# The first feed-forward of a two-layer kernel: another order of its turns and joins, one group of bias products per step, both norms on ScalarE

## The reference

```python
x = layernorm(x + attn0(x))              # 16 heads of 16, causal; ctx @ Wp.T + bp
# first feed-forward, 8 experts, top 2, all experts computed for all tokens:
probs = softmax(x @ router_w + router_b)
gates = top-2 of probs, divided by their sum, 0 elsewhere          # (tokens, 8)
expert_out = gelu(x @ expert_w[e] + expert_b[e])                   # tanh form
x = layernorm(x + (sum_e gates[:, e] * expert_out[e]) @ out_w + out_b)
x = layernorm(x + attn1(x));  x = layernorm(x + ffn1(x))
layernorm(x) = (x - mean) / sqrt(var + 1e-5)
```

## Time and profile before

| | |
|---|---|
| median of 3 runs | 1004.56 us (1003.43 to 1004.66) |
| the profiled execution's own time | 1002.59 us |
| its span, first to last instruction | 1000.7 us |
| mean granted TensorE clock | 0.969 of full speed |
| busy, share of the span | PE 89%, PEld 54%, DVE 72%, ACT 51%, POOL 38% |
| first expert product to last one before the second attention's scores | 280.9 to 454.0 us |

### The profile page before, as it was taken

How to read it: one execution, slowest core, us unless ns; L and a number is a source line. 1 busy time by engine, 2 the same in 40 slices (tenths; PEclk the granted TensorE clock), 3 DMA queues, 4 the chain that set the end, 5 groups by cost and what they waited for, 6 DMA issues and landing times.

```text
span 1000.7 us, 22546 instructions
## 1 busy us (share of the span) xinstructions
PE 889.1 (89%) x8457; PEld 540.2 (54%) x8457; DVE 717.9 (72%) x1955; ACT 515.4 (51%) x1201; POOL 381.5 (38%) x729
## 2 busy tenths in 40 slices
PE   5897989997488989988999999999999999898796
PEld 2444544553334444345565676676667666676464
DVE  4776777676467786758999888888888888422646
ACT  3566657765224343436666555555555655314342
POOL 3543444544335545442333332333233333100455
PEclk8899999999779999999999999999999999999999
DMA  7233222320000000003667565556565555300011
GB/s 268 83 81 85 66 54 65 87 29 7 1 1 1 1 1 1 1 1 68 118 124 122 98 103 97 105 99 102 92 107 98 101 99 99 67 1 1 1 43 43
DMA packets 210428, 65.64 MB, mean 66 GB/s; under 512 B 203008, under 2 KB 206608, under 8 KB 210192
## 3 DMA queue, kind: packets, MB, share of 16 engines
q1 hardware_dynamic: 210320, 64.19, 32.4%
HBM read 17.92 MB, written 4.19 MB: 22 GB/s over the span
## 4 chain that ended last, share of the span: by engine, by line
PE 58%; DVE 17%; ACT 7%; issue 6%; POOL 5%; DMA 5%; SPq 1%; POOLq 0%; DVEq 0%; ACTq 0%
PE bank L411 13%; PE bank L413 12%; PE bank L412 12%; DMA att<-w_lo 4%; PE bank L755 3%; ACT scr L890 3%; PE bank L538 3%; PE bank L757 3%; PE bank L756 3%; DVE scr L1167 2%; ACT att L936 2%; PE bank L459 2%; POOL scr L1706 2%; DVE w_lo L1249 2%; DVE stats L1295 1%
## 5 line engine op out<-in xcount | busy, mean ns | idle before, releaser
L980 ACT ACTIVATE att<-att,nm 128x512 f32<-128x512 f32 (+3 forms) x256 | 141.5, 553 | 103.8 <-DVE nm L1238 102.5
L411 PE MATMUL bank<-w_hi,scr 128*128 128x256 bf16 (+1 forms) x576 | 174.2, 302 | 17.0 <-DVE scr L1167 14.3
L413 PE MATMUL bank<-w_hi,scr 128*128 128x256 bf16 (+1 forms) x576 | 173.8, 302 | 0.0
L412 PE MATMUL bank<-w_lo,scr 128*128 128x256 bf16 (+1 forms) x576 | 173.6, 301 | 0.0
L890 ACT ACTIVATE scr<-bank 128x256 bf16<-128x256 f32 (+3 forms) x208 | 110.4, 550 | 113.4 <-PE bank L757 44.6
L1167 DVE TENSOR_TENSOR scr<-bank,scr 128x256 bf16<-128x256 f32 (+1 forms) x144 | 75.2, 536 | 73.3 <-ACT scr L890 73.1
L1238 DVE CUSTOM_DVE_ANT_0 att<-bank,consts 128x512 f32<-128x512 f32 (+3 forms) x256 | 113.3, 483 | 15.0 <-PE bank L413 15.0
L936 ACT ACTIVATE att<-bank 128x512 f32<-128x512 f32 (+1 forms) x192 | 90.6, 525 | 61.3 <-PE bank L522 60.7
L1225 DVE TENSOR_REDUCE nm<-bank 128x1 f32<-128x512 f32 (+3 forms) x256 | 110.4, 483 | 13.7 <-PE bank L483 13.2
L1741 POOL TENSOR_SCALAR wqkv_hi<-att,rr 128x512 bf16<-128x512 f32 (+3 forms) x128 | 65.6, 532 | 139.0 <-DVE rr L1255 139.0
L1741 POOL TENSOR_SCALAR w_hi<-att,rr 128x512 bf16<-128x512 f32 (+3 forms) x128 | 65.6, 532 | 105.1 <-DVE rr L1255 105.1
(11 more groups left out here) (177 smaller groups left out, 2129.4 us busy)
## 6 DMA issues: line engine op xcount, KB each, us to landing
scr<-wall_in SPq DMA_DIRECT2D x19, 512.0 KB, 4.9
x_tok<-x_tok_in SPq DMA_DIRECT2D x1, 2048.0 KB, 9.4
v_by_token<-scr SPq DMA_DIRECT2D x16, 128.0 KB, 1.8
scr<-v_by_token SPq DMA_DIRECT2D x16, 128.0 KB, 3.3
scr<-x_t_in SPq DMA_DIRECT2D x3, 512.0 KB, 5.9
out<-x_tok SPq DMA_DIRECT2D x3, 512.0 KB, 3.0
scr<-wqkv_in SPq DMA_DIRECT2D x2, 384.0 KB, 3.6
att<-w_hi SPq DMA_TRANSPOSE x32, 3.4
```

The lines of the kernel that those rows point to most:

```text
L411: pe.matmul(out, l_hi, r_hi, start=start, stop=False, skip_group_check=check)
L412: pe.matmul(out, l_hi, r_lo, start=False, stop=False, skip_group_check=check)
L413: return pe.matmul(out, l_lo, r_hi, start=False, stop=stop, skip_group_check=check)
L980: last = act.activation(at, at, ACT.Exp, bias=nm[:, j % 2, qt:qt + 1], scale=-1.0, accum_out=rs[:, j % 2, qt:qt + 1])
```

## The change

It does six things. (1) The four bias products of a step become one group, behind the six products of `experts(n, 0)`: each takes its own quarter of the array's rows (32 q to 32 q + 2), three of them open the banks of calls 1 to 3, the last closes bank 4. PE waits for all four gelus of the step before ahead of the group. (2) The bias rows therefore lie at four partition offsets, and SP moves them with 12 DMAs in place of 3. (3) The turns come in the order x1, cc, cm, x2. PE: x1, experts 0 with the group, first_project, experts 1, cc, experts 2, cm, experts 3, x2, second_project. (4) DVE's order is new: low x1, mix 0, joined 2 of tile n-2 (one step later than before), join_halves(n-1) (moved from the end of the step before), joined 1, low cc, mix 1, low cm, mix 2, context, low x2. (5) Both norms go from DVE (subtract, multiply) to ACT (one activation, scale 1/sqrt, bias -mean/sqrt), norm 1 before gelu 2 and norm 2 before gelu 3; POOL computes the bias with a third small instruction per norm, and does norm 2's numbers first in a step. (6) The router's exponential goes between gelu 0 and gelu 1.

```diff
-TURN_LEADS = (("x1", LEAD), ("x2", -2), ("cm", -1), ("cc", LEAD + 2))
+TURN_LEADS = (("x1", LEAD), ("cc", LEAD + 2), ("cm", -1), ("x2", -2))
...
-            for i in range(3):
-                sp.dma_start(eb3[i:i + 1, :], eb_p[:, i, :]).then_inc(eb_moved, 16)
+            for p in range(4):
+                for i in range(3):
+                    sp.dma_start(eb3[32 * p + i:32 * p + i + 1, :], eb_p[4 * p:4 * p + 4, i, :]).then_inc(eb_moved, 16)
...
             def experts(t, p):
-                hold(pe, m["ge"], 4 * (t - 1) + p + 1)
                 out = bank[4 + p][:, :]
-                pe.matmul(out, ones_b[0:3, :], eb3[:, p * 512:(p + 1) * 512], start=True, stop=False)
+                if p == 0:
+                    hold(pe, m["ge"], 4 * (t - 1) + 1)
                 for k in range(KE):
...
-                               w_hi[:, cs], w_lo[:, cs], False, k == KE - 1)
+                               w_hi[:, cs], w_lo[:, cs], p == 0 and k == 0, p > 0 and k == KE - 1)
+                if p == 0:
+                    hold(pe, m["ge"], 4 * t)
+                    for q in (1, 2, 3, 0):
+                        rows = slice(32 * q, 32 * q + 3)
+                        last = pe.matmul(bank[4 + q][:, :], ones_b[rows, :], eb3[rows, :], start=(q > 0), stop=(q == 0),
+                                         tile_position=(32 * q, 0))
                 last.then_inc(m["f"], 1)
...
# ACT, new; norm(t, which) is gone from DVE, where it was one tensor_scalar
+            def norm(t, which):
+                rows = x_tok[:, t * E:(t + 1) * E]
+                slot = 2 * (which - 1) + t % 2
+                act.wait_ge(m[f"rstd{which}"], t + 1)
+                act.activation(rows, rows, ACT.Identity, bias=shift[:, slot:slot + 1], scale=rstd[:, slot:slot + 1]
+                               ).then_inc(m[f"x{which}"], 1)
...
# ACT, a step after: x1 high, gelu 0, [router_exp], gelu 1, cc high, norm(n+6, 1), gelu 2,
#                    cm high, norm(n-2, 2), gelu 3, x2 high
+                if 0 <= n + LEAD + 1 < NT:
+                    norm(n + LEAD + 1, 1)
+                if here:
+                    gelu(n, 2)
+                if 0 <= n - 1 < NT:
+                    turned_high("cm", n - 1)
+                if 0 <= n - 2:
+                    norm(n - 2, 2)
...
# DVE, a step after
                 if here:
                     mix(n, 0)
+                if 0 <= n - 2:
+                    joined(n - 2, 2)
+                if 0 <= behind < NT:
+                    join_halves(behind)
                 if 0 <= ahead < NT:
                     joined(ahead, 1)
...
# POOL
+            def scale_and_shift(t, which):
+                pool.wait_ge(m[f"agg{which}"], t + 1)
+                mix_chain(pool.tensor_scalar(var_e[:, col], mv[:, slot, 1:2], EPS, 1.0, ALU.add, ALU.mult))
+                hold(pool, m[f"x{which}"], t - 1)
+                mix_chain(pool.tensor_tensor(rstd[:, col], var_e[:, col], neg_half[:, one], ALU.pow))
+                pool.tensor_scalar(shift[:, col], mv[:, slot, 0:1], rstd[:, col], -1.0, ALU.mult, ALU.mult
+                                   ).then_inc(m[f"rstd{which}"], 1)
             def mix_step(n):
+                if 0 <= n - 2:
+                    scale_and_shift(n - 2, 2)
                 if 0 <= n + LEAD + 1 < NT:
+                    scale_and_shift(n + LEAD + 1, 1)
                 if 0 <= n < NT:
                     mix(n, 2)
...
                     pool.tensor_tensor(rows, rows, outb_bc[:, :], ALU.add).then_inc(m["xb"], 1)
+                if 0 <= n < NT:
+                    mix(n, 3)
```

More of the change, by code:

```diff
@@ L689, in _ @@
                     experts(n, 0)
-                if 0 <= n + 4 < NT and (n + 4) % TT == TT - 1:
+                routed = 0 <= n + 4 < NT and (n + 4) % TT == TT - 1
+                if routed:
                     logits((n + 4) // TT)
-                if 0 <= n - 2:
-                    turn_mix("x2", n - 2)
-                routed = 0 <= n + 4 < NT and (n + 4) % TT == TT - 1
                 if 0 <= ahead < NT and not routed:
@@ L710, in _ @@
                 if 0 <= behind < NT:
-                    second_project(behind)
+                    turn_mix("cm", behind)
                 if n == NT:
@@ L715, in _ @@
                     experts(n, 3)
+                if 0 <= n - 2:
+                    turn_mix("x2", n - 2)
+                if 0 <= behind < NT:
+                    second_project(behind)
             l1_project("q", 0, 1)
@@ L964, in l0_slot @@
                         if 0 <= n + LEAD:
+                            norm(n + LEAD, 1)
                             turned_high("x1", n + LEAD)
@@ L1295, in joined @@
                 chain(dve.bn_stats(stats[:, slot, :], rows))
+                hold(dve, m[f"rstd{which}"], t - 1)
                 dve.bn_aggr(mv[:, slot, :], stats[:, slot, :]).then_inc(m[f"agg{which}"], 1)
-            def norm(t, which):
-                rows = x_tok[:, t * E:(t + 1) * E]
-                slot = 2 * (which - 1) + t % 2
-                dve.wait_ge(m[f"rstd{which}"], t + 1)
-                dve.tensor_scalar(rows, rows, mv[:, slot, 0:1], rstd[:, slot:slot + 1], ALU.subtract, ALU.mult
-                                  ).then_inc(m[f"x{which}"], 1)
             def sums_inverse(half):
@@ L1371, in join_halves @@
                 dve.wait_ge(m["psum"], (NX - DVE_X - 1) * (t + 1))
-                dve.wait_ge(m["mul"], MIX * t + DVE_X)
-                dve.tensor_tensor(comb[t % 2], comb[t % 2], pc[t % 2], ALU.add).then_inc(m["mul"], 1)
+                dve.wait_ge(m["mul"], DVE_X * (t + 1))
+                dve.tensor_tensor(comb[t % 2], comb[t % 2], pc[t % 2], ALU.add).then_inc(m["join"], 1)
             def route(b):
@@ L1440, in _ @@
                     mix(n, 1)
-                if 0 <= ahead < NT:
-                    norm(ahead, 1)
-                if 0 <= behind < NT:
-                    joined(behind, 2)
                 if routed:
                     choose_first((n + 4) // TT)
+                if 0 <= behind < NT:
+                    turned_low("cm", behind)
+                if n == NT:
+                    l1_low("v", 0)
                 if here:
                     mix(n, 2)
+                if routed:
+                    choose_second((n + 4) // TT)
+                    gate((n + 4) // TT)
                 if 0 <= n + LEAD + 3 < NT:
                     context(n + LEAD + 3)
-                if n == NT:
-                    l1_low("v", 0)
-                if 0 <= behind < NT:
-                    norm(behind, 2)
-                if routed:
-                    choose_second((n + 4) // TT)
-                if routed:
-                    gate((n + 4) // TT)
-                if here:
-                    join_halves(n)
+                if 0 <= n - 2:
+                    turned_low("x2", n - 2)
             l1_low("q", 0, 1)
@@ L1694, in mix @@
                 if p == 2:
-                    hold(pool, m["mul"], MIX * (t - 1))
+                    hold(pool, m["join"], t - 1)
                     if t % TT == 0:
```

63 lines of the change are left out of this document (25 added, 38 removed).

## The result

| | before | after |
|---|---|---|
| median (lowest to highest) | 1003.99 us of 6 runs (1002.44 to 1005.36) | 1008.35 us of 6 runs (1007.62 to 1010.28) |
| the profiled execution's own time, its span | 1002.59, 1000.7 | 1007.9, 1006.0 |
| mean granted TensorE clock | 0.969 | 0.955 |

A forecast was written before the change was run, and what follows sets the result against it. The prediction took a loop through PE, gelu 3, POOL and DVE's join as the bound, 10.4 us a full step. Feed-forward -9.1, issues +5.6 and first norm -1.6 gave -5.1, so 1004.56 became 999.5 us, range 990 to 1009.

The forecast's parts named there:

- The new loop: Full feed-forward steps: gelu 0, DVE's joins, POOL, norm 1, gelu 2, norm 2, x2 turn, experts 0; 10.4 us a step.
- the four bias products run side by side: PE's group in each step: 0.4 us in place of 1.64, a gain of 1.2 of PE's time a step.
- nine more issues: SP's bias-row DMAs at the start of the feed-forward: last landing 9 x 0.62 = 5.6 us later.
- rival 4: Start of the feed-forward: the additional DMA issues cost nothing, 994 us; chance 0.08.
- I keep one fall of the clock as before saw it, 1.3: Feed-forward steps: one clock fall of 1.3 us kept, turning 10.4 us less into 9.1 less.
- rival 1: PE's gaps before x2: clock falls in steps 2 to 9, 1.5 x 8 = 12 us, giving 1010; chance 0.18.
- the gain at the start: Early steps: first norm on ACT takes 0.5 plus 0.3 for POOL's third instruction, against 2.42 on DVE; 1.6 us less.
- the later early norms: Early steps, norms after the first: moving them to ACT comes out even.
- the last routed pair: Feed-forward steps 11 and 12, with routing: forecast at 17.5 us together.
- the old loop: Kernel before, join to join through PE, gelu 3, POOL and DVE: 10.38 us, with four bias products costing 1.64.
- The forecast's price for the new order: Feed-forward to the second attention: 162.7 against 173.1 us, 10.4 less; 9.1 less after one clock fall.
- the end: Steps 13 to 15 and the way to the second attention: 34.3 us against 36.2.

The follow-up runs named there:

- three_issues: The change with the bias rows moved by three strided DMAs in place of twelve; 1002.99 us, 0.9984 of the kernel before.
- fill_gap: The change with twelve idle 256-column products on PE ahead of the x2 turn in each step from n = 2; 1004.34 us, 0.9998 of the kernel before.
- group_only: The kernel before with only the bias products as a group of four and SP's twelve issues; 1007.46 us, 1.0027 of the kernel before, expected about 997.
- norm1_late_and_wait: The change with norm 1 behind norm 2 on ACT and PE's bias-row wait just ahead of the first group; 978.47 us, 0.9739 of the kernel before.
- best: The change with norm 1 behind norm 2, the bias-row wait ahead of the first group, and joined 1 ahead of joined 2 and the join; 987.26 us, 0.9825.
- join_moved_only: The kernel before with only the join of tile n-1 moved behind mix 0 of step n; 1008.16 us, 1.0038 of the kernel before.

## Why the prediction failed

The measured 1008.35 us lie just inside the range of 990 to 1009, which was to take in a clock that falls in most gaps. The direction was wrong: faster had a chance of 0.63, slower 0.26.

**Right.** The new loop, its links and its length (10.25, forecast 10.4) and that PE would stand still before x2 (2.1 to 2.6 us, forecast 2.6). That the four bias products run side by side (0.40). That nine more issues cost 5.6 (5.5 in the trace, 6.3 by three_issues), and rival 4, that they cost nothing, is refuted. Without clock falls the steps come out almost as summed: 0 to 9 were forecast at 103.5 us, and fill_gap takes 102.8.

**Wrong, the largest step:** "I keep one fall of the clock as before saw it, 1.3". In after the clock falls behind the gaps of steps 2, 4, 8 and 9 and behind one of 2.42 us in step 11, not behind those of steps 3, 5, 6 and 7, and the falls before step 10 alone took 5.9 us, by fill_gap. This is rival 1 at half its price: it put a fall into each of eight steps and 1.5 us on each. The rows had shown one fall in two such gaps; that rate times eight gaps of 1.5 us is 6, close to what came, though two gaps are too few to give a rate and the match is partly luck. The forecast took one fall for all eight gaps. (By its own numbers the sign turns at the fifth such fall, not at the fourth: 4 x 1.5 - 1.3 is 4.7, less than 5.1.)

**Right in mechanism, halved by the clock: the gain at the start.** Forecast 1.6 less; it was 0.85 less in the change's profile and 1.65 in that of three_issues, whose clock fell there as in before. Another 0.5 was lost again by step 0: the norm on ACT took 0.60, not 0.5, and the shift (0.27) stands ahead of it. The forecast had the later early norms come out even.

**Wrong: the last routed pair.** Steps 11 and 12 were forecast at 17.5 and took 19.9. PE waits 2.42 us there, ahead of 416.11, for the low part of cm behind DVE's router pieces, a wait that the sum had left out for this step, and the fall of the clock follows it. With the clock full and the gap filled in part, fill_gap ran step 11 1.7 us faster, so most of the 2.4 is the fall.

**Wrong, without effect on the sum: the old loop.** It was said to run through PE and the bias products. group_only shows that it closes on DVE and POOL. The forecast's price for the new order did not use that route, so its number stood; that was luck. The expectation for group_only did use it and was 10 us off.

In all, the feed-forward was to be 9.1 shorter and is 0.9 shorter in the profiled execution. The 8.2 between are, by its own steps: to step 7 3.4 more than forecast (the experts of step 0 at half clock, which the sum had at full, 1.2, the falls of steps 2 and 4 most of the rest), steps 7 to 12 5.4 more (7 to 9 3.0, the last pair 2.4), the end 0.8 more, less the 1.3 counted. The end after the scores is 1.7 shorter and was not forecast; its code is the same in all thirteen kernels, whose profiles have it at 544.8 to 549.7 us, so this is no effect of the change that one profile could show. Nor are the first 2.7 us, as said above.

## What to carry to other kernels

When an order is changed, write down every loop that runs over an in-order engine, the new ones above all: here an instruction that nobody needed soon (norm 1) stood ahead of ones that everything needed (gelu 2, norm 2), and moving it back by three places was worth 17.5 us, nearly four times what the change lost. Place a one-time wait where its data are first used, and count the issues of small DMAs, not only their bytes. A stop of PE that recurs must be priced with what the clock does behind it, at the rate the rows show; filling it with idle products, where PE is not the bound, is a cheap test of that and sometimes a cure.

## What the hardware showed that was not expected

How often the clock falls behind a stop of PE. Between 290 and 450 us of the two kernels and of all runs but fill_gap, PE stood still 42 times for 1.6 to 2.3 us and was granted less than full clock in the 2 us behind it 12 times; of 32 stops of 2.4 us and more 26 were followed by such a fall. Among the 42 the longer ones did not fare worse: 10 of the 24 up to 1.95 us were followed by a fall, 2 of the 18 from 2.09 to 2.24. That is a rate in this kernel, not a rule: gaps of 2.95 us stayed without one (twice in norm1_late_and_wait), gaps of 1.64 had one (twice in best), and no run here settles what tells them apart. norm1_late_and_wait has four such stops where the change has ten.

The mean clock of the first 40 us differed between executions of equal code, 0.75 to 0.83, and at the first context copy of the early steps the thirteen profiles lay up to 3.1 us apart. Small changes should be read from where the code of two kernels first differs.

An activation of 256 columns with two pointers took 0.60 us, as long as a copy or a gelu of 512 columns (0.60), while the plain copy of 256 took 0.38. The Trainium skill (ScalarE: Activation LUTs, "What ACT_TABLE_LOAD costs") gives 280 ns + 0.833 ns a column + 93 ns for the second pointer, 0.59. By that the norm has its price from the page, and the trace agrees within 0.02 us.

The price of a change of the product's height. In the trace of join_moved_only, which has the four single bias products, PE's weight load waits 0.17 us or more ahead of one and 0.23 behind it, both put down to "issue":

```profile
333.80 0.09 PEld L627 LDWEIGHTS bank<-scr,ones_b 3*128 3x128 bf16 x1 [0.17 <-issue]
...
334.11 0.10 PEld L410 LDWEIGHTS bank<-w_hi,scr 128*128 128x128 bf16 x1 [0.23 <-issue]
```

The group has 0.42 ahead and 0.23 behind (after, 364.29), once a step. What it saves is three of these changes, and the three products beside them.
